# Output and feed-forward matmuls as 64-row halves of 256 columns, with the attention values copied out at a pair's end

## What is computed

```python
c_kv = h @ W_dkv + b_dkv
c_q = h @ W_dq + b_dq
k = concat([k_base, rotary(h @ W_kr + b_kr)])    # 16 heads x 64
v = (c_kv @ W_uv + b_uv).reshape(bsz, seq, H, DH)
q = concat([q_base, rotary(c_q @ W_qr + b_qr)])
scores = einsum('bqhd,bkhd->bhqk', q, k) / sqrt(DH)
attn = softmax(scores, axis=-1)
out = einsum('bhqk,bkhd->bqhd', attn, v)
x = layernorm(h + out.reshape(bsz, seq, H * DH) @ W_o + b_o)
w = simulate_quantize_int4(kernel)
y = einsum('bsd,df->bsf', x, w) + bias
lora = einsum('bsr,rf->bsf', einsum('bsd,dr->bsr', x, a), b)
x = layernorm(x + y + lora)
```

## Time and profile before

| | us |
|---|---|
| median of 3 runs | 2162.8 |
| lowest and highest | 2161.38, 2320.59 |
| profiled execution | 2158.53 |
| its span, first to last instruction, core 6 | 2157.0 |
| spans of the 8 cores | 2140.2 to 2157.0 |
| ScalarE busy | 2016.5 |
| TensorE busy (matmuls) | 1938.3 |
| VectorE busy | 602.7 |
| GpSimd busy | 256.6 |

### The profile page before, as it was taken

The page is one execution under the profiler, slowest core; times in us unless marked ns, Lnnn a source line. Parts: engine busy times, 40 slices in busy tenths (PEclk is TensorE's granted clock), DMA queues, the critical chain, the costliest instruction groups (busy, mean ns, idle before and its releaser), DMA issues.

```text
span 2157.0 us, 61016 instructions; the slowest of 8 cores (2140.2 to 2157.0 us)
## 1 busy us (share of the span) xinstructions
PE 1938.3 (90%) x22544; PEld 708.4 (33%) x22544; DVE 602.7 (28%) x1084; ACT 2016.5 (93%) x2177; POOL 256.6 (12%) x303
## 2 busy tenths in 40 slices
PE   5977888989999999998999999999999999999976
PEld 2422333333333333333333333333333333333323
DVE  2731411232223322222222322323222322322224
ACT  2689999989999999998999999999999999999973
POOL 2000000110011110110111100211111100211021
PEclk9999999999999999999999999999999999999998
DMA  9772300121122211221121211312121311323121
GB/s 166 164 148 80 107 23 27 51 92 43 36 83 67 87 45 53 71 71 69 41 93 50 99 36 36 103 54 81 45 92 48 102 31 41 102 85 118 41 70 39
DMA packets 78681, 155.69 MB, mean 72 GB/s; under 512 B 16192, under 2 KB 46912, under 8 KB 78400
## 3 DMA queue, kind: packets, MB, share of 16 engines
q1 hardware_dynamic: 64672, 106.86, 15.5%
q0 software_dynamic: 13728, 44.93, 8.7%
...
## 4 chain that ended last, share of the span: by engine, by line
ACT 69%; issue 16%; PE 6%; DMA 3%; DVE 2%; ACTq 2%; SPq 1%; POOL 0%; DVEq 0%; POOLq 0%
ACT Psb L1004 69%; ACTq L998 2%; DMA wbuf<-hG 1%; DMA rbc<-rec 1%; SPq L495 1%; PE PS L742 1%; PE PS L916 1%; PE PS L858 1%; PE PS L944 1%; DMA osb<-hG 1%; PE PS L729 1%; PE PS L879 1%; PE PS L774 1%; PE PS L769 1%; PE PS L754 1%
## 5 line engine op out<-in xcount | busy, mean ns | idle before, releaser
L1004 ACT ACTIVATE Psb<-PS 128x1024 bf16<-128x1024 f32 x2048 | 1933.9, 1025 | 34.8 <-PE PS L858 22.5
L858 PE MATMUL PS<-Qsb,Ksb 64*128 64x512 bf16 x4096 | 804.0, 387 | 149.4 <-ACT Psb L1004 138.5
L879 PE MATMUL PS<-Psb,Vsb 128*32 128x512 bf16 x8192 | 634.1, 386 | 0.5 <-ACT Psb L1004 0.5
L858 PEld LDWEIGHTS PS<-Qsb,Ksb 64*128 64x128 bf16 x4096 | 212.9, 93 | 702.5 <-issue 696.4
L889 PE MATMUL PS<-Psb,ones_sb 128*32 128x256 bf16 x8192 | 404.1, 274 | 3.5 <-issue 3.5
L889 PEld LDWEIGHTS PS<-Psb,ones_sb 128*32 128x32 bf16 x8192 | 221.7, 97 | 224.2 <-issue 8.1
L1154 DVE TENSOR_TENSOR X<-PS,X 128x512 f32<-128x512 f32 x112 | 77.5, 692 | 625.5 <-PE PS L835 330.0
L879 PEld LDWEIGHTS PS<-Psb,Vsb 128*32 128x32 bf16 x8192 | 127.9, 94 | 236.5 <-issue 236.5
L831 PE MATMUL PS<-wbuf,osb 128*128 128x512 bf16 x448 | 135.6, 384 | 0.0
L802 PE MATMUL PS<-wbuf,osb 128*128 128x512 bf16 x448 | 135.6, 384 | 0.0
L1126 DVE COPY rec<-PS 128x256 f32<-128x256 f32 x64 | 27.1, 423 | 344.9 <-PE PS L889 344.9
...
## 6 DMA issues: line engine op xcount, KB each, us to landing
...
rbc<-rec SPq DMA_DIRECT2D x512, 32.0 KB, 1.8
...
```

The source lines that it names most:

```text
L858: m = pe.matmul(PS[:, b0 + 512 * hh:b0 + 512 * (hh + 1)], Ksb[rows, k0:k0 + 128], Qsb[rows, 512 * p:512 * (p + 1)], tile_position=(64 * hh ...
L879: pe.matmul(PS[32 * j:32 * (j + 1), b0:b0 + 512], Vsb[:, v0:v0 + 32], Psb[:, p0 + 512 * (j // 2):p0 + 512 * (j // 2 + 1)], start=first and ...
L1004: act.activation(Psb[:, 1024 * (g % 4):1024 * (g % 4 + 1)], PS[:, 1024 * (g % 2):1024 * (g % 2 + 1)], AF.Exp, scale=0.125).then_inc(sem["e ...
```

## The change

- A group of `o` or `f` is now a quarter of 256 columns, two slots of four row blocks c. Each 128x128 block is two matmuls of 64 rows by 128 columns, 256 columns moving, in the position of the scores' tiles. The upper half accumulates in bank 7 (columns 0 to 255), the lower one in bank 4 or 5, whichever the running pair doesn't use. The rank-16 term is one more 64-row matmul in the quarter's second slot.
- VectorE adds a quarter in two additions of 256 columns, the second after the first, and takes the statistics after each second quarter.
- Since bank 4 or 5 has to be free, VectorE copies the pair's values to xs (512 columns) right after the sums, at k=0, and the normalisation reads xs. TensorE's background groups and the next `values` wait for that copy (`pv_free`), the `values` also for the additions of the groups before (`groups_by`).
- The planner keeps `o` and `f` to slots 4 to 28 of a pair (a second slot up to 30), starts `o` at 12, steps on by 2.6, and from the rounding puts two slots in one place where the window opens. `rope` stands right after `qr`.

Cut to its core:

```diff
+    def acc(r, pb):
+        b0 = 2048 + 512 * pb if r else 3584
+        return PS[:, b0:b0 + 256]
...
+                for q in range(4):
+                    for i in range(2):
+                        seq.append((o_lo, ("o", qt, sub, q, i)))
+                    if sub and q == 1:
                         seq.append((0, ("tr", qt, sub - 1)))
...
         for lo, st in seq:
             t = max(t, lo)
-            when[st] = 2 * int(t / 2 + 0.5)
+            slot = 2 * int(t / u / 2 + 0.5)
+            if st[0] in ("o", "f"):
+                if st[4]:
+                    slot = min(slot, slot0 // NKC * NKC + NKC - 2)
+                else:
+                    while not 4 <= slot % NKC <= NKC - 4 or used.get(slot, 0) >= u:
+                        slot += 2
+                    slot0 = slot
+            used[slot] = used.get(slot, 0) + 1
+            when[st] = slot * u
             at(T, when[st], st)
-            t += 2.8
+            t = max(t, when[st] - 2) + 2.6
...
+                    if i == 0:
                         pe.wait_ge(sem["ev_misc"], misc_of(st))
+                        pe.wait_ge(sem["pv_free"], g // NKC)
...
+                        for r in range(2):
+                            rows = slice(64 * r, 64 * (r + 1))
+                            m = pe.matmul(acc(r, pb), osb_tok(qt, sub, c)[rows, :],
+                                          wbuf[rows, w0:w0 + 256], start=(c == 0),
+                                          stop=(c == 7 and (r == 1 or not f)),
+                                          tile_position=(64 * r, 0))
...
                 if first and P >= 2:
-                    pe.wait_ge(sem["nrm_done"], P - 1)
+                    pe.wait_ge(sem["pv_free"], P - 1)
+                if first and P - 1 in groups_by:
+                    pe.wait_ge(sem["ev_misc"], groups_by[P - 1])
...
                     dve.tensor_copy(rec[:, :], PS[:, 3072:3328]).then_inc(sem["den_free"], 1)
+                    if P:
+                        dve.wait_ge(sem["nrm_done"], P)
+                    dve.tensor_copy(xs[:, :], bank(4 + P % 2)).then_inc(sem["pv_free"], 1)
...
-                    dve.tensor_tensor(osb_pair(qt, p), bank(4 + P % 2), rbc[:, :], op=ALU.mult
+                    dve.tensor_tensor(osb_pair(qt, p), xs[:, :], rbc[:, :], op=ALU.mult
...
-                    dve.tensor_tensor(Xh(n, half), bank(7), Xh(n, half), op=ALU.add
+                    dve.tensor_tensor(Xq(n, q), acc(0, 0), Xq(n, q), op=ALU.add
+                                      ).then_inc(sem["add_a"], 1)
+                    dve.wait_ge(sem["add_a"], 4 * n + q + 1)
+                    dve.tensor_tensor(Xq(n, q), acc(1, idle_bank[st]), Xq(n, q), op=ALU.add
                                       ).then_inc(sem["ev_misc"], 1)
```

103 lines of the change are left out of this document (51 added, 52 removed).

## The result

| | before | after |
|---|---|---|
| median of all executions in the same comparison (us) | 2162.1 | 2289.6 |
| lowest and highest of the changed kernel | | 2267.95, 2312.16 |
| ratio, 95% interval | | 1.052 [1.046, 1.058] |
| profiled execution, its span (us) | 2158.5, 2157.0 | 2275.0, 2273.4 (core 2) |

Two of the changed kernel's four executions (2304.2 and 2312.2 us) and one of the four of the kernel before ran with one die at a lower granted clock; without these the means are 2271.5 and 2159.8 us, from which the ratio is taken, so the change costs 112 us.

What follows compares the result with a forecast made beforehand. ScalarE's exponentials bound the kernel (93% of the span). 2158.5 - 31 (pitch) + 67 (waits on VectorE) + 8 (clock) + 1 (end) = 2203, set at 2198 us; range 2178 to 2222, over all 2148 to 2230.

Steps and rivals of the forecast that it cites:

- the tail: Last rbc transfer's issue to the normalisation on VectorE; without a weight load beside it, forecast some 2.0 to 2.9 us.
- A slot takes 0.44, the cycle 1.74: TensorE: matmuls after an exponential's scores take 0.44 us; two exponentials' cycle falls from 1.95 to 1.74, under ScalarE's 1.86.
- The pitch goes back to 0.931, 31 us won: ScalarE: exponentials start 0.931 us apart again instead of 0.948 in tiles 1 to 7, winning 31 us.
- Issue from C+4.7 or 5.5, normalisation from C+11.7 to 13.4: SyncE's rbc transfers, then VectorE's normalisation, timed from C, the start of the rec copy; before, C+2.45 and C+10.4.
- Slot 78: TensorE's matmuls after exponential 78's scores wait for slot 76's additions behind the normalisation: 3.0 us, seven tiles.
- Slot 110: TensorE at exponential 110 waits for rotary steps behind the normalisation; chain starts 2.1 later: 2.0 us more, six tiles.
- Slot 238: TensorE at exponential 238 waits for the query evacuation behind the normalisation, wo load beside rbc transfers: 3.3 us, six tiles.
- Slots 206, and 174 of tile 7: TensorE waits behind a cast: 206 1.5 us in six tiles; in tile 7, 174 1.5 and 206 3.5.
- Six drops at 1.4 us: TensorE's granted clock falls to 1.2 GHz after six of thirteen waits of about 3 us: 8 us.
- Rival A: Waits don't cost ScalarE much; 2128.5 us, up to 2120; decides if normalisation starts before C+9.7; chance 0.10, half way 0.08 more.
- Rival B: Long waits cost more, through the wo load at 238 and clock drops after each 3 us wait: 2220 us; chance 0.20.
- Rival C: A slot isn't cheaper on TensorE because 64-row matmuls' weight loads aren't hidden: 0.84 us, about 2260; chance 0.05.

Runs made afterwards that it cites:

- four-edit kernel: Changed kernel, fourth reciprocal at step 4, normalisation at 16, output weights at 246, no two slots in one place: 2131.3 us, 0.981; repeated 2129.1, 0.985.
- the kernel before with its own wait repaired: Kernel before with the normalisation of each pair but a tile's last at step 16 of VectorE's list instead of 12: 2146.8 us, 0.994.
- the run without the overlap: Changed kernel with feed-forward and output weight loads both started after the normalisation of that pair end: 2218.1 us, 1.027 of before.
- with both causes gone: Changed kernel with the fourth reciprocal at step 4 and both weight loads behind the normalisation: 2157.9 us, 0.998 of before.

## Why the prediction was wrong in size

The mechanism was right: VectorE's work behind a later normalisation holds TensorE up at slots 78, 110, 206 and 238. What failed are the sizes of two terms and the gain. The waits at slots 110 and 238 stood in the sum with 12 and 20 us, and these pairs grew by 30.4 and 41.2, the slow clock behind the waits included; the tail of the eight transfers beside a weight load was priced at 3.5 us or less and took 3.9 to 7.7. The clock stood with six drops and 8 us, and there were 19. And the gain of 31 us is 15 at most. One by one:

- *A slot takes 0.44, the cycle 1.74.* Right for the slot: 0.43 to 0.44 us in the rows above, and scores to scores 0.20 us less than with 128 rows. The whole cycle can't be seen, as the exponentials keep it at 1.86.
- *The pitch goes back to 0.931, 31 us won.* Wrong. Without waits and double places the pitch does come to 0.937 (pairs 1, 4 and 5 of the four-edit kernel: 5.0 us over 0.930 a step in 672 steps), but against the kernel before with its own wait repaired the whole package is worth 15 us in tiles 1 to 7 (1702.8 to 1687.5). And in the changed kernel nothing of it is left: the same pairs stand at 14.1 us, against 11.1 before. The prediction saw the double slots only as something that holds up the fourth reciprocal. It didn't price the slots themselves: 0.32 us in each of three and 0.42 in each of four in a tile (three in tile 7), some 18 us over seven tiles. Nor did it price the new layout, which takes back part of the 40 us that the tiling is worth.
- *Issue from C+4.7 or 5.5, normalisation from C+11.7 to 13.4.* Right for the first transfer, and for the normalisation where no load runs (12.3 to 14.1 ahead of slot 78). Ahead of slot 110 it was C+14.7 to 17.2, ahead of slot 238 C+14.8 to 15.9 in tiles 1 to 6. The tail at slot 110 was read from tile 4, 3.5 us from the last issue to the normalisation, which is the shortest of before's seven (3.5 to 7.4); the earlier trace rows is one of the long ones. In the changed kernel it was 5.4 to 7.7, though the load stands as before to the eight transfers, 4.3 us behind the first. Why most tiles now have the long tail stays open; that the load makes it is shown by the run without the overlap (2.0 to 2.5, tile 7 3.2). At slot 238 the tail was 3.9 to 5.5, where I had allowed for 2.0 to 2.9 from the end of the last issue, 2.6 to 3.5 from its start.
- *Slot 78: 3.0 in seven tiles, 21 us.* Measured 28.3 over before, with the slow exponential behind each wait in it (some 1 us each, 6 in all). The wait itself was priced well.
- *Slot 110: 2.0 more in six tiles, 12 us.* Measured 30.4. This is the largest miss with the next one. Loads behind the normalisation take it from 52.4 to 14.1.
- *Slot 238: 3.3 in six tiles, 20 us.* Measured 41.2. The weight load's share is 15.7 with the late issue still in place; with both causes gone 6.0 are left.
- *Slots 206, and 174 of tile 7: 14 us in all.* Measured 8.8 and 2.7.
- *Six drops at 1.4 us, 8 in all.* 19 stretches at the lower level, 120 us in all, against 3 and 17 before: one behind each wait at slots 78, 110 and 238 of tiles 1 to 6, and one at slot 114 of tile 7. The exponential behind such a wait mostly started 1.95 us after the one before it, so each costs 1 us or more, and there were three times as many as reckoned.
- *Rival A* (the waits don't cost ScalarE much) asked for a normalisation before C+9.7; inside a tile the earliest was C+11.0, but for one at C+9.2.
- *Rival B* was the right one: "the wait at 238 meets the wo load as the one at 110 meets wf, and each wait of 3 us drops the clock". Its price of 2220 was still 52 us low because it put 2 us on six waits, where the extra delay was on twelve, and because it kept the 31 us of gain.
- *Rival C* (the slot isn't cheaper) fell with the 0.44. The rule quoted there from the Trainium skill (TensorE: Matmul & The Clock Gate, Part 3: Packing small matmuls), a weight load overlaps matmuls in flight only if its row group differs, doesn't speak against the 0.43 us after all: in this chain each load goes to the other half than the matmul before it. I had read it too strictly.

Put together, for tiles 1 to 7: forecast were waits of 67, clock 8 and a gain of 31, +44; the trace has +115. Against the four-edit kernel the pairs of the changed one lost 33.2 (slot 78), 48.4 (slot 110, of which 15.2 were in the kernel before too), 43.4 (slot 238), 14.4 (pairs 5 and 6) and 6.0 (pairs 0, 1 and 4), clock and double places included: 130 where 75 stood. Of these 55 us some 21 belong to slot 110, 23 to slot 238 and 12 to slot 78. The gain was 15 and not 31, which makes up the rest.
